# Row gathers cut from two groups to one, and spread over the slabs, in a graph network on one core

## The chip, the cores and the metric

The kernel runs on one core of one Trainium2 chip. The metric is the device time of one launch in microseconds (us); smaller is better. The kernel before takes 3316.73 us, the median of three runs (3312.34 to 3317.65).

## The reference

A graph of 6250 nodes and 200,000 directed edges (sorted by destination) carries 128 features per node. Two networks follow each other, each added to its input and layer-normalised:

```
x = layernorm(x + gru_network(x, edge_weight))
x = layernorm(x + gin_network(x))

gru_network, three layers:
    m = x @ weight[l]
    agg = segment_sum(m[src] * edge_weight[:, None], dst)
    gi, gh = agg @ w_ih.T + b_ih, x @ w_hh.T + b_hh
    r = sigmoid(i_r + h_r); z = sigmoid(i_z + h_z); n = tanh(i_n + r * h_n)
    x = (1 - z) * n + z * x
gin_network, three layers:
    x = relu((x + segment_sum(x[src], dst)) @ W.T + b)
```

Only layers 2 and 3 of the first network, and the end of its layer 1, are touched by the change.

## The kernel before, in words

**Layout.** Nodes are padded to 49 tiles of 128 (6272). The features stand on the partitions in `xT` (128 x 6272). The 6272 destination nodes are dealt into 14 groups of 448 (`GW`). `Y` holds the node-major copy of `xT`, one 128 x 128 tile per 128 source nodes, which TensorE uses as weights.

**Layer 1 builds the matrix.** The stage goes in 28 spans of 224 destination nodes (`build_span`, `hot_span`, `evac_span`). TensorE builds the dense, weighted adjacency of a span from one-hot products (L1199), ScalarE evicts it (L1602), TensorE uses it at once for layer 1 (L1206), and SyncE stores it to HBM: the weighted strips as `adj_w` in float32, two of 2744 KB a span, and the counts as `adj_h` in float16 for the second network (`store_strips`, L526). The weighted strips of the last `RUN_SPANS` = 4 spans are not stored, since layers 2 and 3 never read them.

**Layers 2 and 3, dense groups.** For groups 0 to 11 (`DENSE` = 12) TensorE multiplies all 49 tiles of `Y` by the group's piece of `adj_w` (`aggregate`, L923: 49 matmuls of 448 columns in float32, each recorded as two). The piece comes in four slabs of 13, 12, 12 and 12 tiles, 2912 or 2688 KB each, into a ring of four slabs. SyncE issues the load of a slab as soon as TensorE has done the last matmul on that slab one group earlier (`s_used`, `dense_slab`, L509). ScalarE evicts the sum (`evac`, L1338), six gate matmuls follow (`gates`, L927; 12 records), and ScalarE and VectorE do the gate arithmetic (`sigmoids`, `mix`, `blend`). The order on TensorE is aggregate(n+1), gates(n), aggregate(n+2), gates(n+1). In layer 2 this is a loop, in layer 3 it is written out, with 7 transposes per pair of groups between (`flip_sums`, L1073).

**Layers 2 and 3, groups 12 and 13 from rows.** Their 896 nodes are 448 pairs. Each pair owns one lane of a run. Per round GpSimd gathers one row of `y_rows` (the HBM copy of `Y`) per lane, 128 rows of 512 B, by an indirect DMA (`fetch_rows`, L828 to L839), into one of ten buffers (`ROW_BUFS`); VectorE multiplies the rows by two weights per lane and adds them to two sums (`add_rows`, L1725; two instructions a round, L1738). Three full runs of 100 rounds and a last, doubled one of 50 make 350 rounds per layer. Finally `flip_runs` (L979) turns the sums into the group's place in PSUM with matmuls against the identity.

**Order of the row work.** VectorE does the rounds in slots between its gate work: 30 before group 0, then 33 after each group's gate arithmetic until 350 are done, so the slots after groups 0 to 8 hold 33 and the one after group 9 holds 23. Within a slot VectorE waits for nothing but the landing of each row and its own previous sums. GpSimd issues ahead until the ten buffers are full and then waits for `s_acc`, VectorE's count of sums. SyncE's queue holds the slab loads alone in this stage, GpSimd's queue the row gathers alone.

Of the kernel before, what the change touches and what calls it, by code (L numbers as in the profile page):

```python
# [10 lines left out]
ALU = mybir.AluOpType  # L11
ACT = mybir.ActivationFunctionType

P = 128
# [15 lines left out]
GROUPS = 14  # L30
# [23 lines left out]
DEALS += [(run, lane + REST, pair, n) for run, lane, pair, n in DEALS if run == RUNS - 1]  # L54
SLOT_FIRST, SLOT_NEXT = 30, 33
# [43 lines left out]
def gnn_program(nc, x, src, dst, firsts, nodes, edges, edge_weight, gnn_w, w_ih, w_hh, b_ih, b_hh,  # L99
# [7 lines left out]
    with ctx:  # L107
# [263 lines left out]
        DENSE = GROUPS - 2  # L371
        SKIPPED = GROUPS - DENSE
        EARLY = len([j for j, (c, n) in enumerate(CHUNKS) if (c + n) * P <= DENSE * GW])
# [280 lines left out]
        def _(pool):  # L654
# [215 lines left out]
        def _(pe):  # L870
# [152 lines left out]
            def last_gru_layer():  # L1023
# [9 lines left out]
                for i in range(DENSE // 2):  # L1033
                    early = range(3 if i == DENSE // 2 - 1 else SLABS)
                    aggregate(n0 + 2 * i + 1, 1, slabs=early, skipped=SKIPPED)
                    if i:
                        flip_sums(i - 1, (6, 7))
                    aggregate(n0 + 2 * i + 1, 1, slabs=range(early.stop, SLABS), skipped=SKIPPED)
# [4 lines left out]
                    if i < DENSE // 2 - 1:  # L1043
                        aggregate(n0 + 2 * i + 2, 0, skipped=SKIPPED)
                        if i == 0:
                            pe.wait_ge(s_sc, 9)
                            pe.transpose(ps[:, 7, 0:P], w_row[:, :], ident[:, :]).then_inc(s_bnd, 1)
                        gates(n0 + 2 * i + 1, 1, 2 * i + 1)
                flip_runs(1, GROUPS - 2)
# [278 lines left out]
        def _(act):  # L1328
# [14 lines left out]
            def evac_runs(layer, group):  # L1343
                bank = group - DENSE
                act.wait_ge(s_flipr, 2 * layer + bank + 1)
                act.wait_ge(s_gate, GROUPS * layer + group + 1)
                act.activation(aggS[bank].rearrange("p (w d) -> p d w", d=WIN),
                               ps[:, bank, 0:GW].rearrange("p (d w) -> p d w", d=WIN), ACT.Copy).then_inc(s_evac, 1)
# [854 lines left out]
```

## Time and profile before

| what | value |
|---|---|
| median of three runs | 3316.73 us |
| span of the profiled execution | 3300.9 us, 15.8 us below the median |
| TensorE busy | 2999.7 us, 91% of the span |
| VectorE, ScalarE, GpSimd busy | 46%, 27%, 30% |
| layer 1 with the matrix | about 0 to 1090 us |
| layer 2 | about 1090 to 1797 us (its last gates overlap layer 3's start) |
| layer 3 of the first network | to about 2480 us |
| second network | to the end |

The profiled execution's own time is not given apart from the median of the runs; span plus 15.8 us stands for it here. A matmul counts as busy for as long as its record lasts, which is longer at the lower clock, so the 91% alone doesn't tell at what pace TensorE moves. "issue" names time in which an engine waited for nothing that the profile shows, and "remote" a release whose sender the profile doesn't show.

### The profile page before, as it was taken

To read this page: it belongs to the slowest core of one execution; us is meant where nothing else is said; L and a number is where in the kernel's file an instruction comes from. 1 tells how busy PE (TensorE), PEld (TensorE's weight loads), DVE (VectorE), ACT (ScalarE), POOL (GpSimd) and SP (SyncE) were. 2 spreads that over 40 slices of the span, in tenths; PEclk is the share of its full clock that TensorE was granted. 3 is DMA by queue.
4 is the path that set the end of the run, shared out by engine and by line. 5 is a ranking of instruction groups with operands and counts; after the bars stand their busy time and mean duration, and the time that the engine had idled before them with its cause. 6 is when DMAs were issued, how large, how long until landed. Compare 5 with 4: busy or idle time off the path is not lost.

```text
span 3300.9 us, 75545 instructions
## 1 busy us (share of the span) xinstructions
PE 2999.7 (91%) x29405; PEld 1914.6 (58%) x29405; DVE 1519.5 (46%) x4507; ACT 904.4 (27%) x2115; POOL 980.1 (30%) x1214
## 2 busy tenths in 40 slices
PE   6999999999999987878789787878889999999998
PEld 5888888888888533434345333434345555555554
DVE  7888888888887233434342343434442001001111
ACT  5666666666665100000001001001022001001111
POOL 3222223222323344655551464554520000000000
PEclk8999999999999988878889888888889999999999
DMA  5655555555532866657577565746656876877885
GB/s 192 266 230 242 231 237 238 236 236 233 242 127 76 343 237 231 252 200 275 184 280 283 220 231 212 267 177 258 223 221 240 306 302 254 304 301 269 299 307 186
DMA packets 150125, 796.32 MB, mean 241 GB/s; under 512 B 19300, under 2 KB 29480, under 8 KB 136200
## 3 DMA queue, kind: packets, MB, share of 16 engines
q1 hardware_dynamic: 119960, 729.87, 56.3%
q0 software_dynamic: 27344, 54.53, 5.7%
q10 hardware_dynamic: 2720, 10.62, 0.8%
q8 instruction: 57, 0.93, 0.1%
q14 instruction: 44, 0.36, 0.0%
HBM read 567.97 MB, written 226.97 MB: 241 GB/s over the span
## 4 chain that ended last, share of the span: by engine, by line
PE 90%; issue 8%; DVE 1%; ACT 1%; DMA 0%; POOL 0%; another core or an unknown queue 0%; ACTq 0%; DVEq 0%; POOLq 0%
PE ps L923 28%; PE ps L1127 24%; PE ps L1206 18%; PE ps L1199 11%; PE ps L933 2%; PE ps L934 2%; PE ps L1219 1%; PE ps L935 1%; PE ps L936 1%; PE ps L1220 1%; PE ps L1106 1%; ACT ring L1602 0%; PE ps L1073 0%; PE ps L1221 0%; PE ps L1222 0%
## 5 line engine op out<-in xcount | busy, mean ns | idle before, releaser
L923 PE MATMUL ps<-ring,Y 128*128 128x448 f32 x2352 | 927.8, 550 | 145.6 <-issue 145.5
L836 POOL DMA_INDIRECT ring<-y_rows,ring x700 | 673.5, 962 | 683.4 <-DVE ring L1738 410.7
L923 PEld LDWEIGHTS ps<-ring,Y 128*128 128x128 f32 x2352 | 453.6, 193 | 594.8 <-issue 594.8
L1127 PE MATMUL ps<-ring,Y 128*128 128x448 f16 x4116 | 780.6, 352 | 0.0
L1602 ACT ACTIVATE ring<-ps 128x392 f16<-128x392 f32 (+1 forms) x1568 | 654.1, 504 | 303.6 <-PE ps L1199 297.1
L1127 PEld LDWEIGHTS ps<-ring,Y 128*128 128x128 f16 x4116 | 402.7, 98 | 373.8
L1206 PE MATMUL ps<-ring,Y 128*128 (+1 forms) x2744 | 613.9, 366 | 3.4 <-issue 2.9
L1738 DVE SCALAR_TENSOR_TENSOR ring<-ring 128x128 f32<-128x128 f32 x1384 | 402.1, 347 | 350.3 <-DMA ring<-y_rows,ring 223.8
L1206 PEld LDWEIGHTS ps<-ring,Y 128*128 128x128 f32 x2744 | 490.5, 189 | 19.3 <-issue 4.1
L1199 PEld LDWEIGHTS ps<-shared 64*128 64x128 bf16 x18816 | 341.3, 94 | 132.7 <-ACT ring L1602 87.0
L1199 PE MATMUL ps<-shared 64*128 64x49 bf16 (+1 forms) x18816 | 391.1, 191 | 22.4 <-issue 10.3
L2050 DVE TENSOR_TENSOR shared<-shared 128x400 bf16<-128x400 bf16 x1176 | 396.0, 391 | 0.0
L1341 ACT ACTIVATE shared<-ps 128x448 f32<-128x448 f32 x24 | 13.1, 544 | 1079.0 <-remote 847.8
L2046 DVE TENSOR_TENSOR shared<-iota_lo,shared 128x1024 bf16<-128x1024 bf16 x392 | 279.1, 712 | 0.0
L1914 DVE TENSOR_REDUCE x_tops<-xT x28 | 17.4, 620 | 482.3 <-ACT xT L1508 482.3
L1508 ACT ACTIVATE xT<-ps,bcur,unscale 128x448 f32 (+1 forms) x42 | 30.4, 725 | 682.1 <-PE ps L1127 682.1
L2044 DVE TENSOR_TENSOR shared<-iota_key,shared 128x400 bf16<-128x400 bf16 x392 | 148.1, 378 | 119.4 <-PE ps L1199 110.6
L1682 DVE SCALAR_TENSOR_TENSOR shared<-ps,bhh,shared 128x448 f32<-128x448 f32 x28 | 19.2, 684 | 329.0 <-ACT shared L1358 329.0
L731 POOL DMA_INDIRECT shared<-in_edges,take_now x60 | 61.8, 1029 | 360.0 <-PE ps L1199 357.3
L933 PE MATMUL ps<-shared,wT 128*128 128x448 f32 x112 | 78.5, 760 | 54.6 <-issue 53.8
L1880 DVE TENSOR_TENSOR shared<-shared,ps 128x384 f32 (+3 forms) x14 | 8.7, 622 | 228.5 <-PE ps L1142 228.1
L934 PE MATMUL ps<-xT,wT 128*128 128x448 f32 (+1 forms) x112 | 72.1, 720 | 27.6 <-issue 27.6
(188 smaller groups left out, 1309.6 us busy)
## 6 DMA issues: line engine op xcount, KB each, us to landing
ring<-adj_w SPq DMA_DIRECT2D x72, 2688.0 KB
adj_w<-ring SPq DMA_DIRECT2D x48, 2744.0 KB, 12.2
ring<-adj_h SPq DMA_DIRECT2D x42, 2800.0 KB, 9.4
ring<-adj_h SPq DMA_DIRECT2D x42, 2688.0 KB, 9.1
adj_h<-ring SPq DMA_DIRECT2D x56, 1372.0 KB, 5.0
ring<-adj_w SPq DMA_DIRECT2D x24, 2912.0 KB
ring<-y_rows,ring POOLq DMA_INDIRECT x700
y_rows<-Y ACTq DMA_DIRECT2D x2, 2560.0 KB, 10.9
```

Of the source, the lines that this page charges most:

```text
L836: pool.indirect_dma_start(out=run_rows[:, i % ROW_BUFS, :], out_offset=None, in_=y_rows, in_offset=bass.IndirectOffsetOnAxis(ap=run_edges[ ...
L923: mm = pe.matmul(ps[:, bank, 0:GW], Y[:, h, :], slab(s)[:, :, h - h0, :], start=(h == 0), stop=(last and h == TILES - 1))
L933: pe.matmul(ps[:, bank, 0:GW], wT[:, c, :], aggS[par], start=True, stop=False)
L934: pe.matmul(ps[:, bank, 0:GW], wT[:, 3 + c, :], xg, start=False, stop=True)
L1127: mm = pe.matmul(ps[:, par, 0:GW], part[:, h, :], counts_slab(par, s)[:, :, h - h0, :], start=(h == 0 and part is Y_high), stop=(h == TILE ...
L1199: mm = pe.matmul(sums, hot_lo[slots, buf, w, :], rhs, start=(part == 0), stop=(part == WPARTS - 1))
L1206: mm = pe.matmul(ps[:, AGG_BANK, 0:SPAN], Y[:, h, :], strip_w[:, bass.ds(slot, 1), :, h, :].rearrange("p o b c -> p (o b) c"), start=(h == ...
L1602: act.activation(strip[:, :, c0:c0 + UNIT * WIN].rearrange("p h (d j) -> p d h j", d=WIN), psum_unit(a)[:, :, kind, :, :].rearrange("p d j ...
L1738: add = dve.scalar_tensor_tensor(out=run_sums[:, run, d, :], in0=run_rows[:, buf, :], scalar=weight, in1=run_sums[:, run, d, :], op0=ALU.m ...
L2044: dve.tensor_tensor(in_pairs(hot[:, buf, :, 0, :]), every_window(iota_key, WIDE), values(par, 0, k, WIDE), ALU.is_equal).then_inc(s_hot, 1)
L2046: dve.tensor_tensor(in_pairs(hot_lo[:, buf, :, :]), every_window(iota_lo, P), values(par, 1, k, P), ALU.is_equal).then_inc(s_hot, 1)
L2050: dve.tensor_tensor(in_pairs(hot[:, buf, :, 1 + part, :]), in_pairs(hot[:, buf, :, 0, :]), values(par, 2 + part, k, WIDE), ALU.mult).then_ ...
```

## The change

`RUN_SPANS` goes from 4 to 2 and `DENSE` from 12 to 13: only group 13 is summed from rows, group 12 is a dense group like the others, and so two more spans of layer 1 have their weighted strips stored. The row group now has two runs of 100 rounds (128 and 96 lanes; the rest of the second run's lanes have weight 0), so a layer has 200 rounds and not 350. The doubled last run with its extra instructions goes. The slots hold 24 rounds before group 0 and 16 after each of groups 0 to 10, and each slot is cut in three parts (8, 8, 8 and 6, 5, 5): ahead of the second and third part VectorE waits until TensorE has used the first and the second slab of the group that it is running (`paced_rows`). The tails of both layers are reordered for the one more dense group.

```diff
@@ constants
-RUN_SPANS = 4
+RUN_SPANS = 2
 ROW_BUFS = 10
 RUN_PAIRS = RUN_SPANS * 112
-RUN_LENGTHS = [RUN, RUN, RUN, RUN // 2]
-RUN_STARTS = [0, RUN, 2 * RUN, 3 * RUN]
+RUN_LENGTHS = [RUN, RUN]
+RUN_STARTS = [0, RUN]
 RUNS = len(RUN_LENGTHS)
 REST = RUN_PAIRS - (RUNS - 1) * P
-assert 2 * REST == P
+assert 0 < REST < P and REST % 32 == 0
 ROUNDS = sum(RUN_LENGTHS)
 SPAN_PAIRS = 112
 CUTS = sorted({*range(0, RUN_PAIRS + 1, SPAN_PAIRS), *range(0, RUN_PAIRS, P), RUN_PAIRS})
 DEALS = [(a // P, a % P, a, b - a) for a, b in zip(CUTS, CUTS[1:])]
-DEALS += [(run, lane + REST, pair, n) for run, lane, pair, n in DEALS if run == RUNS - 1]
-SLOT_FIRST, SLOT_NEXT = 30, 33
+SLOT_FIRST, SLOT_NEXT = 24, 16
+SLOT_CUTS = [0, 6, 11, SLOT_NEXT]
+FIRST_CUTS = [0, 8, 16, SLOT_FIRST]
...
-        DENSE = GROUPS - 2
+        DENSE = GROUPS - 1
...
@@ gpsimd
-            pool.tensor_scalar(run_base[REST:P, :, RUNS - 1], run_base[REST:P, :, RUNS - 1], float(-WIN * REST), None, ALU.add)\
-                .then_inc(s_rbase, 1)
+            pool.memset(run_base[REST:P, :, RUNS - 1], -1.0).then_inc(s_rbase, 1)
             pool.wait_ge(s_rbase, 2)
+            pool.memset(run_take[:, :], 0).then_inc(s_half, 1)
...
             def deal_takes():
+                pool.wait_ge(s_half, 1)
...
-                pool.tensor_scalar(run_take[REST:P, RUNS - 1:RUNS], run_take[REST:P, RUNS - 1:RUNS], float(RUN // 2), None, ALU.add)\
-                    .then_inc(s_half, 1)
-                pool.wait_ge(s_half, 1)
...
@@ tensor
-            def flip_runs(layer, group):
-                bank, q0 = group - DENSE, (group - DENSE) * GW // WIN
-                last = [run for run in range(RUNS) if run * P < q0 + GW // WIN][-1]
-                pe.wait_ge(s_acc, WIN * (ROUNDS * layer + RUN_STARTS[last] + RUN_LENGTHS[last]))
-                pe.wait_ge(s_evac, GROUPS * layer + group - WIN + FREE + 1)
+            def flip_runs(layer):
+                pe.wait_ge(s_acc, WIN * ROUNDS * (layer + 1))
+                pe.wait_ge(s_evac, GROUPS * layer + GROUPS - 1 - WIN + FREE + 1)
                 for d in range(WIN):
-                    for run in range(RUNS - 1):
-                        lo, hi = max(run * P, q0), min((run + 1) * P, q0 + GW // WIN)
-                        if lo < hi:
-                            c = d * GW // WIN + lo - q0
-                            mm = pe.matmul(ps[:, bank, c:c + hi - lo], run_sums[:, run, d, :], ident[:, lo - run * P:hi - run * P],
-                                           start=True, stop=True)
-                    if group == GROUPS - 1:
-                        c = (d + 1) * GW // WIN - REST
-                        for half in range(2):
-                            lanes = slice(half * REST, (half + 1) * REST)
-                            mm = pe.matmul(ps[:, bank, c:c + REST], run_sums[:, RUNS - 1, d, :], ident[:, lanes],
-                                           start=(half == 0), stop=(half == 1))
+                    for run in range(RUNS):
+                        lanes = P if run < RUNS - 1 else REST
+                        c = d * GW // WIN + run * P
+                        mm = pe.matmul(ps[:, 1, c:c + lanes], run_sums[:, run, d, :], ident[:, 0:lanes], start=True, stop=True)
                 mm.then_inc(s_flipr, 1)
...
-                aggregate(DENSE - 1, 1, slabs=range(SLABS - 1))
-                gates(DENSE - 2, 0, DENSE - 2)
-                aggregate(DENSE - 1, 1, slabs=range(SLABS - 1, SLABS))
-                flip_runs(0, GROUPS - 2)
-                gates(DENSE - 1, 1, DENSE - 1)
-                flip_runs(0, GROUPS - 1)
+                aggregate(DENSE - 2, 1)
+                gates(DENSE - 3, 0, DENSE - 3)
+                aggregate(DENSE - 1, 0, slabs=range(SLABS - 1))
+                gates(DENSE - 2, 1, DENSE - 2)
+                aggregate(DENSE - 1, 0, slabs=range(SLABS - 1, SLABS))
+                flip_runs(0)
                 node_chunks(2, 0, 2, THIRD_BANKS)
...
+                aggregate(n0 + DENSE - 1, 0, slabs=range(SLABS - 1, SLABS), skipped=SKIPPED)
+                flip_runs(1)
                 first_messages(0, 2)
-                gates(n0 + DENSE - 1, 1, DENSE - 1)
-                flip_runs(1, GROUPS - 1)
+                gates(n0 + GROUPS - 2, 0, GROUPS - 2)
                 first_messages(2, 4)
-                gates(n0 + GROUPS - 2, 0, GROUPS - 2)
-                first_messages(4, 6)
                 gates(n0 + GROUPS - 1, 1, GROUPS - 1)
-                first_messages(6, 10)
+                first_messages(4, 10)
                 flip_sums(PAIRS - 2, (4, 5))
...
@@ vector
-                return max(0, min(ROUNDS, SLOT_FIRST + SLOT_NEXT * slot))
-
-            def add_rows(layer, slot, part=range(SLOT_NEXT)):
+                return min(ROUNDS, SLOT_FIRST + SLOT_NEXT * slot) if slot >= 0 else 0
+
+            def add_rows(layer, slot, part):
...
+            def paced_rows(layer, slot):
+                cuts = SLOT_CUTS if slot >= 0 else FIRST_CUTS
+                for k, (lo, hi) in enumerate(zip(cuts, cuts[1:])):
+                    if k:
+                        dve.wait_ge(s_used, SLABS * (1 + layer * DENSE + slot + 2) + k)
+                    add_rows(layer, slot, range(lo, hi))
...
+                paced_rows(0, -1)
                 for g in range(GROUPS):
                     gru_group(g, g)
-                    add_rows(0, g)
+                    if g < DENSE - 2:
+                        paced_rows(0, g)
```

## Rows read from the trace of the kernel before

**Rows 1.** The page: busy shares, the chain by engine, and the costliest group.

```profile
PE 2999.7 (91%) x29405; PEld 1914.6 (58%) x29405; DVE 1519.5 (46%) x4507; ACT 904.4 (27%) x2115; POOL 980.1 (30%) x1214
...
PE 90%; issue 8%; DVE 1%; ACT 1%; DMA 0%; POOL 0%; another core or an unknown queue 0%; ACTq 0%; DVEq 0%; POOLq 0%
...
L923 PE MATMUL ps<-ring,Y 128*128 128x448 f32 x2352 | 927.8, 550 | 145.6 <-issue 145.5
```

**Rows 2.** The chain in order of time, layer 2: start us, us, what.

```profile
1101.78 42.85 PE ps L923 x114
...
1196.71 36.49 PE ps L923 x97
...
1310.58 34.58 PE ps L923 x92
...
1713.10 27.81 PE ps L923 x74
```

**Rows 3.** The same chain: full pace, and one of six equal gate pieces.

```profile
1740.91 0.75 PE ps L933 x2
...
1797.11 36.84 PE ps L923 x98
```

**Rows 4.** The same chain in layer 3.

```profile
1882.34 36.08 PE ps L923 x96
...
2411.57 27.81 PE ps L923 x74
2439.38 0.77 PE ps L1073 x7
```

**Rows 5.** Windows: us, busy of PE, PEld, DVE, ACT, POOL; PEclk, DMA share, GB/s.

```profile
1310.00:1345.00 35.00, 35.00 (x94) 17.67 (x93) 20.52 (x67) 1.74 (x3) 21.81 (x23) 1.00 0.87 338
1345.00:1363.00 18.00, 5.85 (x9) 2.01 (x8) 1.41 (x5) 0.00 (x0) 9.90 (x11) 0.62 0.16 42
...
1713.00:1770.00 57.00, 57.00 (x182) 30.93 (x181) 24.38 (x64) 10.48 (x19) 12.67 (x13) 1.00 0.85 341
...
2550.00:2600.00 50.00, 50.00 (x266) 25.87 (x265) 1.86 (x3) 2.17 (x3) 0.00 (x0) 1.00 0.82 310
```

**Rows 6.** Timeline of GpSimd, first and last gather of one slot's burst.

```profile
1316.49 1.09 POOL L836 DMA_INDIRECT ring<-y_rows,ring  x1 [15.24 <-DVE ring L1738]
...
1357.00 0.95 POOL L836 DMA_INDIRECT ring<-y_rows,ring  x1 [0.30 <-issue]
```

**Rows 7.** Timeline of SyncE's slab loads and of ScalarE's eviction, the same group.

```profile
1329.54 0.37 SPq L512 DMA_DIRECT2D ring<-adj_w  x1
...
1363.11 0.99 SPq L512 DMA_DIRECT2D ring<-adj_w  x2
...
1363.20 0.54 ACT L1341 ACTIVATE shared<-ps 128x448 f32<-128x448 f32 x1 [49.73 <-remote]
```

**Rows 8.** Timeline of GpSimd: a burst of 13 gathers, and layer 2's first.

```profile
1718.78 1.08 POOL L836 DMA_INDIRECT ring<-y_rows,ring  x1 [16.01 <-DVE ring L1738]
...
1734.08 1.02 POOL L836 DMA_INDIRECT ring<-y_rows,ring  x1 [0.30 <-issue]
...
1119.20 0.94 POOL L836 DMA_INDIRECT ring<-y_rows,ring  x1 [41.85 <-DMA y_rows<-Y]
```

**Rows 9.** The chain: the matmuls of `flip_runs` for group 12, and the last of group 13.

```profile
1754.44 0.86 PE ps L989 x8
...
1759.85 0.45 PE ps L989 x4
...
1761.18 0.39 PE ps L995 x4
```

**Rows 10.** Timeline of ScalarE: one such instruction a span, here spans 20, 23, 26.

```profile
786.95 0.45 ACT L1554 ACTIVATE shared<-ps 128x336 f32<-128x336 f32 x1 [0.72 <-PE ps L1182]
...
897.47 0.45 ACT L1554 ACTIVATE shared<-ps 128x336 f32<-128x336 f32 x1 [0.72 <-PE ps L1182]
...
1007.69 0.45 ACT L1554 ACTIVATE shared<-ps 128x336 f32<-128x336 f32 x1 [0.72 <-PE ps L1182]
```

More of the change, by code:

```diff
@@ L370, in gnn_program @@
         LAST_ACT = 5
-        DENSE = GROUPS - 2
+        DENSE = GROUPS - 1
         SKIPPED = GROUPS - DENSE
-        EARLY = len([j for j, (c, n) in enumerate(CHUNKS) if (c + n) * P <= DENSE * GW])
+        EARLY = len([j for j, (c, n) in enumerate(CHUNKS) if (c + n) * P <= (GROUPS - 2) * GW])
         MASK_STEPS = WIN + 3
@@ L1033, in last_gru_layer @@
                 for i in range(DENSE // 2):
-                    early = range(3 if i == DENSE // 2 - 1 else SLABS)
-                    aggregate(n0 + 2 * i + 1, 1, slabs=early, skipped=SKIPPED)
+                    last = i == DENSE // 2 - 1
+                    aggregate(n0 + 2 * i + 1, 1, slabs=range(3), skipped=SKIPPED)
                     if i:
                         flip_sums(i - 1, (6, 7))
-                    aggregate(n0 + 2 * i + 1, 1, slabs=range(early.stop, SLABS), skipped=SKIPPED)
+                    aggregate(n0 + 2 * i + 1, 1, slabs=range(3, SLABS), skipped=SKIPPED)
                     if i == 0:
@@ L1042, in last_gru_layer @@
                     gates(n0 + 2 * i, 0, 2 * i)
[L1043 to L1049, printed above, removed]
+                    aggregate(n0 + 2 * i + 2, 0, slabs=range(SLABS - 1 if last else SLABS), skipped=SKIPPED)
+                    if i == 0:
+                        pe.wait_ge(s_sc, 9)
+                        pe.transpose(ps[:, 7, 0:P], w_row[:, :], ident[:, :]).then_inc(s_bnd, 1)
+                    gates(n0 + 2 * i + 1, 1, 2 * i + 1)
+                aggregate(n0 + DENSE - 1, 0, slabs=range(SLABS - 1, SLABS), skipped=SKIPPED)
+                flip_runs(1)
                 first_messages(0, 2)
-                gates(n0 + DENSE - 1, 1, DENSE - 1)
-                flip_runs(1, GROUPS - 1)
+                gates(n0 + GROUPS - 2, 0, GROUPS - 2)
                 first_messages(2, 4)
-                gates(n0 + GROUPS - 2, 0, GROUPS - 2)
-                first_messages(4, 6)
                 gates(n0 + GROUPS - 1, 1, GROUPS - 1)
-                first_messages(6, 10)
+                first_messages(4, 10)
                 flip_sums(PAIRS - 2, (4, 5))
@@ L1341, in evac, with evac_runs @@
                 act.activation(by_unit(aggS[par]), natural(ps[:, par, 0:GW]), ACT.Copy).then_inc(s_evac, 1)
[L1343 to L1348, printed above, removed]
+            def evac_runs(layer):
+                act.wait_ge(s_flipr, layer + 1)
+                act.wait_ge(s_gate, GROUPS * layer + GROUPS)
+                act.activation(aggS[1].rearrange("p (w d) -> p d w", d=WIN),
+                               ps[:, 1, 0:GW].rearrange("p (d w) -> p d w", d=WIN), ACT.Copy).then_inc(s_evac, 1)
             def keep_rows(layer, j0, j1):
@@ L1441, in second_gru_layer @@
                     update(2 * i + 1)
+                evac(DENSE - 2, 1)
+                update(DENSE - 3)
                 update(DENSE - 2)
-                evac(DENSE - 1, 1)
-                evac_runs(0, GROUPS - 2)
-                sigmoids(DENSE - 1)
-                evac_runs(0, GROUPS - 1)
-                tanh(DENSE - 1)
+                evac(DENSE - 1, 0)
+                evac_runs(0)
                 take_chunks(2, 0, 2, THIRD_BANKS)
@@ L1468, in last_gru_layer @@
                 update(n0 + 1)
-                with act.Fori(1, DENSE // 2 - 1) as i:
+                with act.Fori(1, PAIRS - 2) as i:
                     n = n0 + 2 * i
@@ L1476, in last_gru_layer @@
                     update(n + 1)
[L1477 to L1482 removed]
+                deviate(PAIRS - 3)
+                evac(n0 + DENSE - 2, 1, SKIPPED)
+                keep_norm(PAIRS - 3, (6, 7))
+                update(n0 + DENSE - 3)
+                update(n0 + DENSE - 2)
+                evac(n0 + DENSE - 1, 0, SKIPPED)
+                evac_runs(1)
                 first_highs(0, 2)
[L1484 to L1487 removed]
                 sigmoids(n0 + GROUPS - 2)
                 tanh(n0 + GROUPS - 2)
[L1490 removed]
+                first_highs(2, 4)
                 sigmoids(n0 + GROUPS - 1)
                 tanh(n0 + GROUPS - 1)
[L1493 removed]
+                first_highs(4, 10)
                 deviate(PAIRS - 2)
@@ L1732, in add_rows @@
                     if r == 0 and layer:
-                        dve.wait_ge(s_flipr, 2 * layer)
+                        dve.wait_ge(s_flipr, layer)
                     for d in range(WIN):
@@ L1844, in last_gru_layer @@
                 sum_group(n0, 0)
-                add_rows(1, 0)
+                paced_rows(1, 0)
                 take_centred_weights(7)
                 sum_group(n0 + 1, 1)
-                add_rows(1, 1)
-                for i in range(1, DENSE // 2 - 2):
+                paced_rows(1, 1)
+                for i in range(1, PAIRS - 2):
                     statistics(i - 1, (6, 7))
@@ L1852, in last_gru_layer @@
                         sum_group(n0 + 2 * i + par, 2 * i + par)
-                        add_rows(1, 2 * i + par)
-                statistics(DENSE // 2 - 3, (6, 7))
-                sum_group(n0 + DENSE - 4, DENSE - 4)
-                add_rows(1, DENSE - 4)
+                        if i < PAIRS - 3 or par == 0:
+                            paced_rows(1, 2 * i + par)
+                last = 2 * (PAIRS - 3) + 1
+                add_rows(1, last, range(SLOT_CUTS[2]))
+                statistics(PAIRS - 3, (6, 7))
+                add_rows(1, last, range(SLOT_CUTS[2], SLOT_NEXT))
                 sum_group(n0 + DENSE - 3, DENSE - 3)
-                add_rows(1, DENSE - 3, range(14))
-                statistics(DENSE // 2 - 2, (6, 7))
-                add_rows(1, DENSE - 3, range(14, SLOT_NEXT))
+                paced_rows(1, DENSE - 3)
                 sum_group(n0 + DENSE - 2, DENSE - 2)
                 first_lows(0, 2)
-                sum_group(n0 + DENSE - 1, DENSE - 1)
+                sum_group(n0 + GROUPS - 2, GROUPS - 2)
                 first_lows(2, 4)
-                sum_group(n0 + GROUPS - 2, GROUPS - 2)
-                first_lows(4, 6)
                 sum_group(n0 + GROUPS - 1, GROUPS - 1)
-                first_lows(6, 10)
+                first_lows(4, 10)
                 statistics(PAIRS - 2, (4, 5))
```

15 lines of the change are left out of this document (1 added, 14 removed).

## Prediction

> **What bounds the kernel now.** The page comes first: TensorE is busy 91% of the span, the chain that ended last lies on it for 90%, and another 8% is "issue", time in which it waited for nothing the profile shows. The costliest group, the aggregation matmuls of layers 2 and 3, carries 145.5 us of such idle time [rows 1]. So the second view is the chain in order of time, to see where that time lies.
>
> In layer 2 the stretches at full pace start at 1196.71, 1310.58 (two groups later) and 1713.10 us [rows 2]; from the first to the last there are nine groups, 516.4 / 9 = 57.38 us each. What TensorE needs for a group is far less: 98 records at full pace take 36.84 us, and six gate pieces of 0.75 us make 4.51 us [rows 3], together 41.35 us. **Each group loses 16.03 us.** In layer 3 nine groups from 1882.34 to 2411.57 us take 58.80 us each, against 41.35 plus half of the 0.77 us of transposes that each pair has [rows 4], 41.74 us: 17.06 us lost per group.
>
> The windows show how. For 35 us TensorE runs 94 records back to back at granted clock 1.00; in the next 18 us it gets through 9, and the granted clock falls to a mean of 0.62, so partly at the lower of its two levels, 1.2 GHz. DMA is not the reason: its share falls from 0.87 to 0.16 in the same stretch. GpSimd goes on gathering, 11 rounds in those 18 us [rows 5]. The gathers of this slot run from 1316.49 to about 1358 us without a pause, 0.95 us plus 0.30 us each [rows 6], and TensorE is back at full pace about five us after the last. The third view is the neighbours' timeline. A slab load that follows TensorE's progress still comes on time at 1329.54 us; the next is due nine us later (24 records), yet it and its follower are issued together at 1363.11 us, when ScalarE's eviction is also released [rows 7]. So TensorE's signals are late, too, and the bound is not any engine's work: **while gathers run without a pause for longer than some 14 to 20 us, signals between engines are late, and TensorE slows visibly 28 us after the burst's start** (1345 less 1316.49). That the gathers cause it is my reading, and it rests on two more rows. The slot after group 9 leaves only 13 rounds to be gathered, from 1718.78 to 1734.08 us [rows 8], and in that window TensorE is busy 57.00 of 57 us although DMA is at 0.85 [rows 5]. And the second network, without gathers, keeps TensorE busy 50.00 of 50 us at more than twice the records per us [rows 5].
>
> **What is lost in all.** Layer 2's first burst starts at 1119.20 us [rows 8] and meets a stall from 1144.63 us (1101.78 + 42.85) to the next full stretch at 1196.71 [rows 2]: 52.1 us for 68 records, which at 0.376 us are 25.6 us, so 26.5 us are lost. With 9 x 16.03 = 144.3 layer 2 loses 170.8 us. Layer 3: from 1797.11 to 1882.34 us [rows 3, 4] lie 158 records (146 of L923, 12 of the gates), 59.4 us of work in 85.2 us, 25.7 us lost; with 9 x 17.06 = 153.5 it loses 179.2 us. Both: **350 us.**
>
> **The change, part by part.**
> - *One more dense group per layer:* 98 records, 36.84 us of TensorE each [rows 3], **+73.7 us**. Its gates existed before.
> - *`flip_runs`:* 24 records before, in 0.86 us for group 12 and 1.72 us for group 13 (1759.85 to 1761.57) [rows 9]; now 8 records, about 0.9 us. **-3.4 us** for both layers.
> - *16 rounds a slot:* 16 x 1.25 = 20 us of gathers per group of 41 us. Because GpSimd is ten rounds ahead, the waits on VectorE hardly split the burst: six buffers come free some 5 us after the gates, five at the end of slab 0 (9.8 us) and five at the end of slab 1 (18.8 us), and each refill takes 6 to 7.5 us. So the burst is some 20 us long and ends about 26 us into the group; TensorE slowed only after 28 us of burst. Late signals within it would only delay a slab load, and slabs have 27 us of room (three slabs of 9.0 us). So I cost the stall of a steady group at nothing: **-350 us.** Its bounds: below nothing, as for the burst of 13; above, in proportion between 13 rounds (nothing) and 33 (16.0 us), 2.4 us in each of 22 slots, +53 us.
> - *First bursts:* 24 rounds and ten ahead make 34 rounds, 42 us, long enough for a stall. Here the new waits matter: they depend on TensorE's own signals, so when these are late VectorE stops, ten buffers fill, GpSimd pauses and the signals catch up. Bounds: nothing, and today's 26 us per layer; I take 10 each, nearer to the short end because of this feedback. **+20 us.**
> - *The added waits:* behind a waiting VectorE lie only its rounds, then `statistics` and the next group's gate arithmetic, needed 36 us into the group; the rounds end by 25. GpSimd waits for `s_acc` as before. Covered by TensorE's group; without that cover the 20 us of gathers would be paid in each group.
> - *Slab loads:* 11.2 MB per 41.4 us are 271 GB/s, with 1.05 MB of rows 297. TensorE ran at full pace beside 338 and 341 GB/s [rows 5]. Nothing; what is late next is nothing of the stream.
> - *Four more strips stored in layer 1:* spans 21 to 23, with these stores, take (897.47 - 786.95) / 3 = 36.84 us, spans 24 to 26, without, 36.74 [rows 10]. Hidden behind TensorE; at most 0.3 us. Fewer list gathers and masks on GpSimd and VectorE, a memset at the start: off the path, a us either way.
> - *Tails:* gates and messages are moved, not added. The wait for the gate arithmetic of group 12 ahead of the gates of group 13 stays, with as much work between. One us either way.
>
> Sum: 3300.9 - 350 + 73.7 - 3.4 + 20 = 3041.2 us of span, and with the 15.8 us by which the median stands above the span **3057 us**, 0.922 of before.
>
> **The rivals.**
> *The stall belongs to the dense group (slower, 6%).* It comes at nearly the same place in each group, after 90 to 97 of 98 records, as if TensorE's own supply of instructions ran dry once a group. Then fewer gathers help nothing and each layer pays one more full group: 3316.7 + 57.4 + 58.8 - 3.4 = 3430 us. Against it: the layer's last group has none [rows 2, 5], and the second network issues faster without it. It decides from 11.7 us of stall per group on (280 us of expected gain over 24 groups); below that the change still gains.
> The Trainium skill ("Runtime: NRT & Kernel Launch", section "Instruction fetch mechanics") says that instructions are refilled in blocks and that a taken branch out of the current window costs a fetch. By it a loop would stall and written-out code not; layer 2's loop and layer 3's written-out groups lose 16.0 and 17.1 us alike, so the trace speaks against it.
>
> *The stall comes back smaller (still faster, 12%).* The gathers now meet slab loads during 26 of 41 us and TensorE never idles, so late signals might pile up over groups. With 5 to 8 us in 22 slots: 3037 + 110 to 176 = 3147 to 3213 us. For it: today the signals recover only with TensorE and DMA nearly idle. Against it: the slowdown comes 28 us into a steady burst and 25 us into the very first (1144.63 less 1119.20), so nothing is carried over, and 21 of 41 us are now free of gathers against 16 of 57.
>
> *The waits do nothing (same time, within the forecast).* If the number of rounds alone decides, unpaced slots of 16 would do as well; only the first bursts would differ.
>
> **Chances.** Forecast 80%, smaller stall 12%, slower 6%, anything else 2%. The range reaches from 3030 (no first stalls, and the us either way) to 3135 (the 53 us above, the first bursts as today). A measurement of this kernel can tell about 0.2%, 7 us. Faster 0.93, same 0.01, slower 0.06.
>
> **What would show it.** Right: groups of 41.4 to 42 us in the chain of both layers, 98-record stretches running into the gates without "issue", PEclk 1.00 throughout, four slab loads a group 9 to 14 us apart, ScalarE's eviction no longer released "remote", a short stall at most near the second group of each layer. Wrong: stretches that still break off after 90-odd records, or gathers that still run into late slab loads.

## The result, and the profile after

The changed kernel takes 3024.25 us (four runs, 3022.96 to 3024.35), the kernel before beside it 3316.09 us (3312.34 to 3317.65). The ratio is 0.9116 [0.9104, 0.9129]: 292 us faster. The forecast was 3057 us in a range from 3030 to 3135: right in direction and in what takes the stall away, but 33 us too slow, and the range missed the time by 6 us. The larger surprise came later: in seven of the ten sets of runs of this study the kernel before takes 2940 us, its stall is absent, and there the same change costs 67 us.

The page of the changed kernel: busy shares, granted clock, chain, costliest group.

```profile
PE 2968.0 (98%) x29569; PEld 1921.8 (64%) x29569; DVE 1330.0 (44%) x3889; ACT 904.1 (30%) x2115; POOL 684.3 (23%) x903
...
PE 97%; DVE 1%; issue 1%; ACT 1%; DMA 0%; POOL 0%; ACTq 0%; DVEq 0%; POOLq 0%
...
L922 PE MATMUL ps<-ring,Y 128*128 128x448 f32 x2548 | 963.2, 539 | 0.0
```

Against [rows 1]: "issue" on the chain fell from 8% to 1%, and the idle time before the aggregation matmuls from 145.6 us to nothing, though there are 196 records more. The mean of a record fell from 550 to 539 ns, since none is left at the lower clock.

Its chain in order of time, layer 2, then the start of layer 3:

```profile
1088.44 9.77 PE ps L922 x26
...
1100.51 63.89 PE ps L922 x170
1168.91 36.83 PE ps L922 x98
1210.26 36.83 PE ps L922 x98
...
1660.05 54.88 PE ps L922 x146
1719.67 36.83 PE ps L922 x98
1761.12 27.81 PE ps L922 x74
```

A group now takes 1210.26 - 1168.91 = 41.35 us where it took 57.38 [rows 2]. The first bursts, forecast to cost 10 us a layer, cost nothing: 170 records without a break in layer 2 (114 before the first break in [rows 2]), 146 in layer 3. Three windows, columns as in [rows 5]:

```profile
1088.00:1130.00 42.00, 42.00 (x131) 22.48 (x129) 6.24 (x22) 5.23 (x12) 7.92 (x9) 1.00 1.01 403
1130.00:1165.00 35.00, 35.00 (x95) 17.68 (x94) 11.54 (x40) 0.00 (x0) 23.66 (x25) 1.00 0.84 317
1210.00:1251.00 41.00, 41.00 (x110) 20.71 (x109) 11.82 (x37) 2.28 (x4) 15.51 (x16) 1.00 0.80 296
```

GpSimd, first and last gather of a steady slot: 16 gathers in 20 us, where [rows 6] had 33 in 41.

```profile
1215.93 1.07 POOL L835 DMA_INDIRECT ring<-y_rows,ring  x1 [20.92 <-DVE ring L1719]
...
1235.16 0.94 POOL L835 DMA_INDIRECT ring<-y_rows,ring  x1 [0.30 <-issue]
```

SyncE's slab loads during the first burst, and the sums that VectorE takes up again after its first added wait:

```profile
1127.74 0.38 SPq L513 DMA_DIRECT2D ring<-adj_w  x1
1145.38 10.67 SPq L513 DMA_DIRECT2D ring<-adj_w  x3
...
1145.24 5.34 DVE L1719 SCALAR_TENSOR_TENSOR ring<-ring 128x128 f32<-128x128 f32 x20 [9.84 <-remote]
```

The load after 1127.74 waits for TensorE's next 26 records, 9.8 us, and so was due at about 1137.3; it came at 1145.4, 8 us late. VectorE's first added wait asks for the same count of `s_used`, and VectorE went on at the same moment, 1145.2. TensorE itself ran without a break. So a signal of TensorE was late for two engines here, as it was for SyncE in [rows 7]; but the burst of 18 gathers had ended (last start 1141 us) before the slabs in the ring ran out.

### The profile page after: what moved, and what is told of

The parts are those of the page before. It is cut to its first block, busy times and chain, and to the rows that moved or that the text cites. A ratio compares the mean times of both kernels' runs of the same rounds, so it can differ in the third digit from the quotient of the medians.

```text
span 3022.6 us, 74703 instructions
## 1 busy us (share of the span) xinstructions
PE 2968.0 (98%) x29569; PEld 1921.8 (64%) x29569; DVE 1330.0 (44%) x3889; ACT 904.1 (30%) x2115; POOL 684.3 (23%) x903
## 4 chain that ended last, share of the span: by engine, by line
PE 97%; DVE 1%; issue 1%; ACT 1%; DMA 0%; POOL 0%; ACTq 0%; DVEq 0%; POOLq 0%
PE ps L922 32%; PE ps L1113 26%; PE ps L1192 19%; PE ps L1185 12%; PE ps L932 1%; PE ps L933 1%; PE ps L1205 1%; PE ps L1206 1%; PE ps L935 1%; PE ps L934 1%; PE ps L1092 1%; ACT ring L1583 0%; PE ps L1207 0%; PE ps L1208 0%; PE ps L1168 0%
## 5 line engine op out<-in xcount | busy, mean ns | idle before, releaser
L922 PE MATMUL ps<-ring,Y 128*128 128x448 f32 x2548 | 963.2, 539 | 0.0
L922 PEld LDWEIGHTS ps<-ring,Y 128*128 128x128 f32 x2548 | 483.3, 190 | 469.8 <-issue 469.8
L835 POOL DMA_INDIRECT ring<-y_rows,ring x400 | 386.5, 966 | 690.7 <-DVE ring L1719 486.7
L1192 PEld LDWEIGHTS ps<-ring,Y 128*128 128x128 f32 x2744 | 490.4, 189 | 17.9 <-issue 2.6
L1719 DVE SCALAR_TENSOR_TENSOR ring<-ring 128x128 f32<-128x128 f32 x792 | 216.4, 347 | 197.5 <-issue 88.1
L1343 ACT ACTIVATE shared<-ps,brz 128x448 f32<-128x448 f32 x28 | 17.7, 633 | 142.7 <-PE ps L935 142.7
L693 POOL COPY shared<-shared 112x128 f32<-112x128 f32 x28 | 13.5, 483 | 195.7 <-DVE shared L1959 195.7
```

The costliest lines, as they stand in the source:

```text
L835: pool.indirect_dma_start(out=run_rows[:, i % ROW_BUFS, :], out_offset=None, in_=y_rows, in_offset=bass.IndirectOffsetOnAxis(ap=run_edges[ ...
L922: mm = pe.matmul(ps[:, bank, 0:GW], Y[:, h, :], slab(s)[:, :, h - h0, :], start=(h == 0), stop=(last and h == TILES - 1))
L1192: mm = pe.matmul(ps[:, AGG_BANK, 0:SPAN], Y[:, h, :], strip_w[:, bass.ds(slot, 1), :, h, :].rearrange("p o b c -> p (o b) c"), start=(h == ...
L1719: add = dve.scalar_tensor_tensor(out=run_sums[:, run, d, :], in0=run_rows[:, buf, :], scalar=weight, in1=run_sums[:, run, d, :], op0=ALU.m ...
```

## The experiments

Two facts order this section. In each set the kernel before ran beside the tested ones on the same chip, and it took either 2938 to 2943 us or 3311 to 3320 us, never a time between. In the results nothing but this time tells the two kinds of place apart (the traces show one thing more, in the last section); a chip of the same number, 11, stands on both sides. **"Stalling place"** means below one where the kernel before takes 3311 to 3320 us (three of ten sets, the first measurement among them), **"smooth place"** one where it takes 2940 (seven of ten). The first seven experiments all met smooth places. A "place" is only that: the runs don't show whether it is the chip, the moment or something else that differs. And of the expectations on record, those of `b_few`, `a_slots33_2` and `b_paced_3` give the kernel before as 400 rounds a layer, where it has 350, and that of `a_unpaced_2` gives the first slot as 18 rounds, where it has 24.

### Waits and slots of the changed kernel, smooth place

`a_unpaced`: the changed kernel without the waits between the parts of a slot.

```diff
                 for k, (lo, hi) in enumerate(zip(cuts, cuts[1:])):
-                    if k:
-                        dve.wait_ge(s_used, SLABS * (1 + layer * DENSE + slot + 2) + k)
                     add_rows(layer, slot, range(lo, hi))
```

> The changed kernel without the waits between the parts of a slot; 16 rounds a slot stay. Theory 1 (length of an unbroken burst of gathers decides): steady groups keep 41.4 us, since their burst is one of 16 in both; only the first burst of each layer grows from 18 to 34 rounds, 42 us, and TensorE stalls there by some 17 us in each layer: 3024 + 34 = 3058 us. Theory 2 (the waits on TensorE's slabs are what frees it): stalls come back in the steady groups, 22 times 5 us or more: 3134 us or more. Theory 3 (the sum of rounds decides): 3024 us, also in the first groups.

Measured: 3007.39 us, the kernel before 2939.81 (13 runs); ratio 1.0232 [1.0215, 1.0249].

`a_slots33`: the same, and the long slots of the kernel before.

```diff
-SLOT_FIRST, SLOT_NEXT = 24, 16
+SLOT_FIRST, SLOT_NEXT = 30, 33
```

> The changed kernel (200 rounds, 13 dense groups) with the old slots of 30 and 33 rounds and no waits between parts. Theory 1 (burst length): per layer a first burst of 40 rounds (26 us lost), four of 33 (16 us each) and one of 28 (about 9 us), then groups of 41.4 us: 100 us lost a layer, 3024 + 200 = 3224 us. Theory 3 (the sum of rounds decides, not how they are dealt): about 3024 us. If the stall belongs to more than the gathers, groups after the last round stall, too.

Measured: 3008.08 us; ratio 1.0234 [1.0217, 1.0251].

`a_slots22`: the same with `SLOT_FIRST, SLOT_NEXT = 24, 22`.

> The changed kernel with slots of 24 and 22 rounds and no waits between parts. Theory 1 with a sharp onset (TensorE slows once a burst is longer than 25 to 28 us, and is free about 5 us after its end): a burst of 22 rounds is 27.5 us, so 0 to 5 us lost in seven slots and 17 in the first burst: 3024 + 34 to 104 = 3058 to 3128 us. With a loss in proportion from 13 rounds (none) to 33 (16 us): 7.2 us in each of seven slots, 3024 + 34 + 101 = 3159 us.

Measured: 3007.65 us; ratio 1.0233 [1.0216, 1.0251].

All three are alike, and slower than the kernel before. Neither the waits nor the length of a slot matters here. One window of `a_slots33` shows why:

```profile
1156.00:1200.00 44.00, 44.00 (x118) 22.23 (x117) 24.52 (x82) 2.28 (x4) 33.38 (x35) 1.00 0.83 305
```

GpSimd gathers without a pause (35 rounds in 44 us, the 1.25 us each of [rows 6]), and TensorE stays at full pace: what went with a stall in the first trace goes with none here.

### The kernel before, its slots cut, smooth place

`b_paced` cuts the slots of 30 and 33 rounds in thirds, the second and third waiting for a slab as in the change (`paced_rows` is the change's; the calls in layer 3 are exchanged in the same way).

```diff
+SLOT_CUTS = [0, 11, 22, SLOT_NEXT]
+FIRST_CUTS = [0, 10, 20, SLOT_FIRST]
...
-                    add_rows(0, g)
+                    if g < DENSE - 2:
+                        paced_rows(0, g)
```

> The kernel before (350 rounds, 12 dense groups) with its slots cut in three parts that wait for TensorE's first and second slab; nothing else. Theory 1 with feedback (the waits hang on TensorE's signals, so late signals stop the gathers before TensorE starves): TensorE stays at full pace within a group, but 33 rounds need 41 us plus pauses of some 4 us, so VectorE gets late and a group takes about 51 us: 3316 - 22 x 6 = 3180 us. If the number of rounds alone decides: 3316 us, same as before.

Measured: 2940.19 us; ratio 1.0 [0.9991, 1.001]. Two more runs of the same kernel, `b_paced_2` and `b_paced_3`, met smooth places as well:

> The kernel before with its slots cut in three parts that wait for TensorE's slabs, once more, on whichever chip comes. Where the kernel before takes 2940 us, this one takes the same, as it did. Where it takes 3316 us: theory 1 with feedback says 3180 us or less, since late signals stop the gathers before TensorE starves; if only the number of rounds decides, 3316 us.

> The kernel before (400 rounds a layer, slots of 30 and 33) with each slot cut in thirds that wait for the slabs, as b_paced. On a chip where the kernel before takes 2940 us: 2940 again. On a chip where it takes 3310: if the unbroken run of gathers is what makes the stall, the three parts of 10 or 11 rounds leave TensorE at full pace as the changed kernel's parts of 6 do, and it is 2955 to 2960, so that cutting alone gives the whole gain and halving the rounds (70 us of TensorE's work) was paid for nothing; if the number of rounds in a group is what counts, 33 rounds a group stall it cut or not: 3150 to 3310.

Measured: 2941.75 us beside 2940.83, and 2941.44 beside 2938.99. These are also the only traces of 350 rounds a layer on a smooth place. TensorE's line of the page, and two stretches of the chain, of `b_paced_3`:

```profile
PE 2889.1 (98%) x29405; PEld 1885.8 (64%) x29405; DVE 1515.8 (52%) x4507; ACT 904.4 (31%) x2115; POOL 982.9 (33%) x1214
```

```profile
1276.46 36.83 PE ps L925 x98
1317.80 36.83 PE ps L925 x98
```

41.34 us a group, with all 33 rounds of a slot: what the prediction took for the cost of the row work is nothing here. In layer 3 the chain runs through the gathers and their sums (DMA 7%, VectorE 4%, GpSimd 2% of the span), so there 350 rounds only just fit beside TensorE. Whether cut slots help the kernel before on a stalling place was never measured; layer 2 of `c_split_3` below has to stand for it.

### The changed kernel again, and small loads

`a_again` is the changed kernel itself in another set.

> The changed kernel as it is, once more. In the last four runs the kernel before took 2940 us where it had taken 3316 us, so its stall was absent there. If the stall hangs on the chip and not on the kernel, two answers are possible: where the kernel before takes 2940 us, the changed one is slower than it by about its own added work, 70 us of TensorE less what the old rounds cost, 3007 to 3024 us, ratio 1.02 to 1.03; where the kernel before takes 3316 us, the changed one takes 3024 us, ratio 0.912.

Measured: 3006.92 us, before 2939.62 (7 runs); ratio 1.0231 [1.0214, 1.0248]. So the first set and this one differ not by an edit but by where or when they ran.

`a33_small` adds 32 small loads (128 x 512 B, from `x_keep` into scratch, issued by ScalarE, at most eight in flight) per group of layer 2 to `a_slots33`, to make more DMAs with many small packets.

```diff
+            def small_loads(use):
+                for j in range(32):
+                    act.wait_ge(s_extra[j % 8], 16 * (4 * use + j // 8 + 1))
+                    act.dma_start(scratch[:, j % 8, :], x_keep[:, j * P:(j + 1) * P]).then_inc(s_extra[j % 8], 16)
```

> The changed kernel with slots of 30 and 33 rounds and, in layer 2 alone, 32 more small loads per group from ScalarE's queue (128 rows of 512 B each, up to eight in flight), beside the gathers. Three times as many small transfers and DMA signals in layer 2, the same in layer 3, which serves as control. Theory 1a (late signals come from too many DMA completions for what carries them): layer 2 shows slab loads issued late and TensorE slowing, layer 3 not, over 3030 us where the kernel before takes 2940 us. Theory 1b (it is a property of one chip, or of the gathers' own kind of transfer): both layers keep 41.4 us a group, 3008 us. On a chip where the kernel before takes 3316 us: layer 3 shows the stall of bursts of 33 rounds (16 us each), layer 2 at least that.

Measured: 3006.89 us beside 2941.95. The loads cost nothing and make no stall on a smooth place; of a stalling one it says nothing.

### Gathers almost gone, and slots of 33 without waits, on a stalling place

`b_few`: the kernel before, but of each run of rounds only the first five are gathered and summed. It leaves out 330 of 350 rounds a layer, so most of the sums of groups 12 and 13.

```diff
+KEPT = [i for i in range(ROUNDS) if i % RUN < 5]
+SLOT_FIRST, SLOT_NEXT = 2, 2
...
-                for i in range(ROUNDS):
+                for m, i in enumerate(KEPT):
```

> The kernel before with only the first 5 rounds of each of the four runs gathered and summed: 20 rounds a layer in place of 400 (the other 380 are left out, so most of what groups 12 and 13 add by rows is missing); slots of two rounds. TensorE's work and every slab load stay as before. Theory 1 (the row work and the slab loads collide, but only on the chip of the first measurement): where the kernel before takes 3316 us, this one loses the stall of some 17 us a group, 350 us in all, and takes about 2960; where the kernel before takes 2940, nothing is left to gain, and it takes 2935 to 2941. Theory 2 (the stall of the first chip is one of slab loads or of TensorE itself, rows or not): 3316 there, 2940 elsewhere. Rival for a chip at 2940: rows still cost TensorE small waits spread over the groups; then it is 2900 to 2930.

`a_slots33_2`: `a_slots33` again.

> The changed kernel with slots of 30 and 33 rounds and no waits between their parts, once more. If the stall belongs to unbroken gathers of that length: on a chip where the kernel before takes 3316 us, this one shows the stall again in the groups that still carry rows (6 or 7 groups a layer x 17 us, 200 to 240 us over the changed kernel's 3024), though only 200 rounds a layer are left. If it belongs to the chip only together with 400 rounds a layer: 3024 there. On a chip where the kernel before takes 2940: 3007, as twice before.

Measured, on one chip: the kernel before 3310.96 us, `b_few` **2953.55**, `a_slots33_2` **3236.85**. First `b_few`, a window over three and a half groups, and the group of its aggregation matmuls:

```profile
1100.00:1250.00 150.00, 150.00 (x416) 76.92 (x415) 9.55 (x22) 8.48 (x16) 15.30 (x16) 1.00 0.82 319
```

```profile
L924 PE MATMUL ps<-ring,Y 128*128 128x448 f32 x2352 | 888.4, 539 | 0.0
```

TensorE's instructions and slab loads are those of the kernel before, and the stall is gone: 3310.96 - 2953.55 = 357 us (the prediction had summed 350 from the chain). The changed kernel lies 3024.25 - 2953.55 = 70.7 us above it, which is 73.7 - 3.4 = 70.3 us of added TensorE work, if the two sets are taken as one kind of place.

`b_few` leaves out the gathers and VectorE's sums together. The trace of the kernel before tells them apart, and shows what TensorE does in its stall. TensorE's chain, then VectorE's last sum of the same slot:

```profile
1346.09 0.54 PE ps L923
1346.63 2.26 issue
1348.89 0.54 PE ps L923
1349.43 2.27 issue
1351.69 0.90 PE ps L923
1352.60 1.20 issue
1353.80 0.90 PE ps L923
...
1348.22 0.35 DVE L1738 SCALAR_TENSOR_TENSOR ring<-ring 128x128 f32<-128x128 f32 x1 [0.76 <-issue]
```

VectorE has no sum left after 1348.6 us, but TensorE crawls on for as long as the gathers, which reach to 1358 us, and some 5 us more. So the gathers, rather than the sums, go with the stall. And the crawl itself is not a late signal: these records lie within one slab, where the code of `aggregate` holds no wait, and yet they start 2.1 to 2.8 us apart. The lower clock isn't the reason either, since it makes a record 0.90 us long. What holds TensorE's own instructions back, the profile doesn't show.

Then `a_slots33_2`, whose 200 rounds a layer lie in slots of 33. Windows around the ends of two groups in layer 2, and between them:

```profile
1228.00:1253.00 25.00, 12.87 (x22) 5.25 (x21) 2.15 (x6) 0.69 (x2) 10.38 (x11) 0.66 0.33 110
1253.00:1288.00 35.00, 34.73 (x93) 17.23 (x91) 20.67 (x67) 1.59 (x3) 22.67 (x23) 1.00 0.80 306
1288.00:1311.00 23.00, 11.10 (x19) 4.73 (x19) 1.40 (x4) 0.54 (x1) 9.62 (x10) 0.63 0.32 103
```

The pattern of [rows 5] is back, with the clock at a mean of 0.66 and 0.63, and ends with the rows. 3236.85 - 3024.25 = 213 us more than the changed kernel, though both gather 200 rounds a layer. So it is not the number of gathers in a layer that costs the time.

### Which half of the remedy works: cut slots against short slots

`c_split` asks both in one kernel: layer 2 has slots of 30 and 33 rounds, cut in thirds with the waits; layer 3 has slots of 24 and 16 without waits.

```diff
-SLOT_FIRST, SLOT_NEXT = 24, 16
-SLOT_CUTS = [0, 6, 11, SLOT_NEXT]
-FIRST_CUTS = [0, 8, 16, SLOT_FIRST]
+SLOTS_OF = [(30, 33), (24, 16)]
+CUTS_OF = [([0, 10, 20, 30], [0, 11, 22, 33]), ([0, 24], [0, 16])]
```

> Two questions in one kernel, told apart by layer: the changed kernel with slots of 30 and 33 rounds cut in thirds that wait for the slabs in layer 2, and slots of 24 and 16 rounds with no waits in layer 3. 200 rounds a layer as in the changed kernel. Where the kernel before takes 2940 us: 3007, and nothing is told. Where it takes 3310: the uncut slots of 33 took 17 us more a group in both layers. If what counts is that gathers run unbroken for long, layer 2 here has groups of 41.3 us, and layer 3 too if bursts of 19 us are short enough (3024 in all); if a group's number of rounds counts, layer 2 keeps its groups of 58 us in the first six or seven (3130) and layer 3 has none; if any uncut burst stalls, layer 3 has some 8 us in each of 12 groups (3120).

> As c_split. Where the kernel before takes 2940 us: 3007. Where it takes 3310: gathers unbroken for long are what counts: 3024, no stall in either layer; a group's number of rounds counts: some 3130, stall of 17 us a group in the first groups of layer 2 alone; any uncut burst stalls: some 3120, 8 us a group in layer 3 alone.

> As c_split_2. Where the kernel before takes 2940 us: 3006. Where it takes 3310: 3024 if only long unbroken gathers stall; 3130, in layer 2 alone, if a group's number of rounds counts; 3120, in layer 3 alone, if any uncut burst does.

`a_unpaced_2`, the changed kernel without waits, was sent with `b_paced_3` for the same question:

> The changed kernel (200 rounds a layer, slots of 18 and 16) with no waits between the parts of a slot. On a chip where the kernel before takes 2940 us: 3007 again. On a chip where it takes 3310: if unbroken bursts make the stall once they are some 25 us long, slots of 16 rounds (some 19 us) show little or none: 3024 to 3060; if any unbroken burst does from its first gathers on, the stall is there in each of 11 or 12 groups a layer for about half its 17 us: 3180 to 3240, as with slots of 33.

Measured on smooth places: `c_split` 3006.28 us beside 2941.08, `c_split_2` 3006.03 beside 2941.06, `a_unpaced_2` 3006.57 beside 2938.99; they tell nothing here. `c_split_3` met a stalling place: **3125.61 us** beside 3319.91. Its chain:

```profile
1289.36 35.33 PE ps L922 x94
...
1405.50 35.33 PE ps L922 x94
...
1740.96 34.96 PE ps L922 x93
1775.92 2.16 issue
...
1820.87 36.83 PE ps L922 x98
1862.32 27.81 PE ps L922 x74
1890.90 9.02 PE ps L922 x24
1904.43 36.83 PE ps L922 x98
```

*Layer 2, long slots cut in thirds.* Two groups take 1405.50 - 1289.36 = 116.14 us, 58.07 each, no less than the 57.38 uncut. *Layer 3, short slots uncut.* Two groups take 1904.43 - 1820.87 = 83.56 us, as in the changed kernel's layer 3 (1803.23 - 1719.67 by its chain). So in steady groups **the length of the slot decides, and the waits do nothing**. But the first burst of layer 3, 24 rounds and ten ahead, stalls without its waits: from the layer's start to the next full stretch it takes 1820.87 - 1740.96 = 79.91 us, in the changed kernel 1719.67 - 1660.05 = 59.62. There the waits are worth 20.3 us: in the changed kernel GpSimd stands still for 4.2 us after 18 gathers (1690.18 + 0.94 to 1695.38 us) and then does 16 more, and TensorE never breaks off; here it does 34 in one run. With the same number of gathers, the unbroken run decides. By layers the sum closes: layer 2 (from its first aggregation to layer 3's) 652.39 against 571.61 us, 80.8 more; layer 3's first burst 20.3 more; 101.1 of the 101.4 us between the two kernels.

The same trace dates the stall. GpSimd's gathers, first and last of three bursts:

```profile
1236.08 1.08 POOL L835 DMA_INDIRECT ring<-y_rows,ring  x1 [11.17 <-DVE ring L1719]
...
1276.75 0.94 POOL L835 DMA_INDIRECT ring<-y_rows,ring  x1 [0.30 <-issue]
...
1749.81 0.95 POOL L835 DMA_INDIRECT ring<-y_rows,ring  x1 [302.70 <-DMA y_rows<-Y]
...
1793.73 0.95 POOL L835 DMA_INDIRECT ring<-y_rows,ring  x1 [1.85 <-remote]
...
1827.12 1.08 POOL L835 DMA_INDIRECT ring<-y_rows,ring  x1 [32.44 <-DVE ring L1719]
...
1846.37 0.95 POOL L835 DMA_INDIRECT ring<-y_rows,ring  x1 [0.30 <-issue]
```

SyncE's slab loads around the second of them, and TensorE in the windows before, in and after its stall:

```profile
1759.18 0.37 SPq L513 DMA_DIRECT2D ring<-adj_w  x1
1797.90 0.37 SPq L513 DMA_DIRECT2D ring<-adj_w  x1
```

```profile
1741.00:1775.00 34.00, 34.00 (x91) 17.10 (x91) 10.39 (x36) 0.82 (x3) 19.18 (x20) 1.00 0.80 295
1776.00:1796.00 20.00, 5.96 (x7) 2.10 (x8) 3.91 (x11) 0.00 (x0) 12.33 (x14) 0.61 0.17 46
1820.00:1862.00 42.00, 42.00 (x114) 21.30 (x113) 12.98 (x40) 2.28 (x4) 15.62 (x16) 1.00 0.84 314
```

The first of the bursts has 33 gathers in 41 us: the thirds of a slot of 33 leave no pause, because 33 x 1.25 us fill the group and VectorE finds each slab long used when it comes to the wait. That is why cutting fails there. In the second (34 gathers) TensorE breaks off at 1775.92, 26 us after the first gather, and by its chain goes on without a break from 1796.28, 2.6 us after the start of the last; no slab load is issued between 1759.18 and 1797.90. The third, 16 gathers in 19 us, ends before that point. Between the first and the second lies layer 2's last burst, of 28 gathers (1411.16 to 1446.16): its group takes 1456.53 - 1405.50 = 51.03 us, 9.7 us more than a free one.

## Why the prediction was right, and where it was wrong

**Right, on a stalling place.** *The stall gone, -350 us:* 357 by `b_few`, and the steady groups run at 41.35 us as forecast. *The dense group and `flip_runs`, +73.7 and -3.4:* 70.7 us against `b_few`, 67 us on smooth places, where they are all that the change does. *Gathers make the stall, and the length of their burst decides:* shown by `b_few`, `a_slots33_2` and the first burst of `c_split_3`. *20 us of burst fit under the 28 us:* shown in layer 3 of `c_split_3`. *Waits do hardly anything in a steady slot, but do in the first burst:* shown by `c_split_3`, both halves. One reading behind this was weaker than it looked: ScalarE's eviction at 1363.20 [rows 7] waits for the end of the group's aggregation, whose last record ends at 1361.00, so it was about 2 us late and not, like the slab load issued with it, 25 us. And "signals are late" accounts for the slab loads but not for TensorE's crawl, whose records wait for no signal.

**Wrong, step "First bursts".** It took +20 us, 10 a layer; the cost was 0. The feedback named there works fully: the bursts are 18 gathers (to 1141 us) and not 34, and the slab load that comes 8 us late is still in time. Uncut, the first burst of layer 3 costs 20.3 us (the bound taken was 26).

**Wrong, last step of the sum, "with the 15.8 us by which the median stands above the span".** In the changed kernel the time of the profiled execution is 3024.3 us for a span of 3022.6, 1.7 us around it, and 1.7 to 2.0 in `b_few`, `a_slots33_2` and `c_split_3`; for the kernel before beside these it is 1.8 and 1.7 (3310.96 for 3309.2, 3319.91 for 3318.2). So some 14 of the 15.8 us were the profiled execution being shorter than the timed runs, not time around a span. With both steps put right the sum is 3041.2 - 20 + 1.8 = 3023 us, and 3024.25 was measured. The range had no room for this: its low end kept the 15.8 us as fixed. (Its high end is mis-added: 53 us and first bursts of 26 us a layer give 3142 us, not 3135.)

**Wrong, and not seen at all: the sign.** Everything was priced from one trace, and its largest term exists on only some places. On a smooth place the change takes 3006.92 us against 2939.62, +67 us, near the sum's own +70 for TensorE's work alone; the four timed kernels there, with or without waits, with slots of 16, 22 or 33, agree to within 1.2 us. One trace couldn't show this. What could have warned is that no engine, no queue and no transfer in it explained the stall: it had to be read as "signals are late", which didn't explain TensorE's gaps.

**The rivals.** *The stall belongs to the dense group (3430 us):* refuted, `b_few` issues the same matmuls and has no stall. The Trainium skill's refill of instructions in blocks ("Runtime: NRT & Kernel Launch", "Instruction fetch mechanics") would by itself have left that stall in place too. *The stall comes back smaller (3147 to 3213):* not for this kernel; each burst starts afresh, as nine groups in a row of 41.34 us show (1168.91 to 1540.99 in the chain after). It is what a half-made change would have given: 3236.85 with long slots, 3125.61 with one layer's slots short. *The waits do nothing (same time):* true of the steady slots, false of the first bursts by 20.3 us in the one layer where they were left out.

**What stays open.** What a stalling place is. On both kinds GpSimd issues a gather each 1.25 us; that the signals to SyncE come late only on one is seen, why is not, nor why TensorE's own instructions come slowly. Small loads from another queue were tried on a smooth place alone, so whether only gathers do this is open too. Between 16 and 33 rounds there are two bursts of 20 gathers in layer 2 of `c_split_3`, which lose 2.6 us together, and the one of 28, which loses 9.7; a kernel of such slots wasn't tried there, nor the changed kernel's 16-round slots with layer 2's first burst uncut. Ten sets are too few for a rate. Since the kernel before wins by 67 us on one kind and loses by 292 on the other, no version here beats both everywhere: 350 rounds at 1.25 us fill 437 of a layer's 537 us (1071.96 to 1608.51 in the chain of `b_paced_3`), so it seems that the pauses which the stalling place needs have to be bought with fewer rounds, and these with the dense group. That is argued and not shown: no run spreads 350 rounds with real pauses of 4 us between them.

## What to carry to other kernels

When a stall has no engine, queue or bandwidth behind it in the trace, run the same kernel in several places before paying for its removal; here the remedy costs 67 us where there is nothing to remedy. If it is real, look for the longest unbroken run of small DMAs and make it shorter than the time after which the consumer slows (25 us here): cutting helps only where the cut leaves a real pause (4.2 us was enough here), and at 33 rounds a group it left none. And take the time around a span from the profiled execution's own time, never from a median of other runs.

## What the runs showed of the hardware

**One kernel, two times.** The same kernel took 2938 to 2943 us in seven sets and 3311 to 3320 in three. The stall needs gathers (20 rounds a layer: none; 33 in a row: 16 to 17 us a group), begins 25 to 31 us after a burst's first gather, and for bursts of 33 or 34 ends 2.6 to 6.0 us after the last one's start (all bursts of layers 2 and 3 in the traces of the kernel before, `a_slots33_2` and `c_split_3`). It isn't one wait: TensorE's records come 1.4 to 3.5 us apart.

**Layer 1 is slower there too, without row gathers.** By the chains, layer 2's first aggregation starts at 1088.44 us in the changed kernel on the stalling place (above), and in `a_again`, the same kernel on a smooth one, here:

```profile
1069.56 9.78 PE ps L922 x26
```

That is 18.9 us for the same work in layer 1, and 3024.25 - 3006.92 = 17.3 us between the two times; `b_few` and `c_split_3`, both on stalling places, start at 1090.66 and 1088.57, while the kernel before with cut slots (`b_paced_3`, smooth) starts at 1071.96. So nearly all that the changed kernel still loses there lies in layer 1. The loss is spread over the stage: in the same 200 us of it, first in the changed kernel on the stalling place and then in `a_again`, TensorE is short of work for 1.3 us at full clock, or not at all:

```profile
400.00:600.00 200.00, 198.72 (x4291) 173.54 (x4291) 175.25 (x488) 135.55 (x332) 52.07 (x84) 1.00 0.57 233
400.00:600.00 200.00, 200.00 (x4356) 175.74 (x4355) 178.24 (x490) 137.22 (x336) 55.43 (x89) 1.00 0.58 239
```

All five traces from stalling places show the first picture (198.70 to 198.86 us busy in this window) and all eleven from smooth ones the second (200.00), so a trace tells the two kinds apart. Why layer 1 is slower there stays open.
